# One transformer block on one core: the written order of four engines laid anew, and both ends of the program

## The reference, cut to what matters

```
x = x + layernorm(attention(layernorm(x)))          # q, k get a position table; causal softmax; Wo
x = x + layernorm(tanh(layernorm(x) @ W @ A1 @ A2 + bias))
attention: qkv = x @ Wqkv.T ; scores = q k.T / 8, masked ; probs = softmax ; (probs v) @ Wo.T
```

## Time and profile before

| what | before |
|---|---|
| median of three runs | 561.74 us |
| the profiled execution, its own time | 561.25 us |
| span of its trace (first to last instruction) | 559.4 us |
| busy: PE / PEld / DVE / ACT / POOL | 537.3 / 455.6 / 469.5 / 409.4 / 398.9 us |
| chain of work that ended last: PE share | 92% |
| granted TensorE clock, mean | 0.987 |
| load of a batch of x, 128 KB, issue to landing, median | 2.2 us |
| scores of batch 1, second pair, idle PE before, waiting for `qk` from DVE (L641) | 1.00 us |

### The profile page before, as it was taken

How to read it: one execution, slowest core, us unless ns; L and a number is a source line. 1 busy time by engine, 2 the same in 40 slices (tenths; PEclk the granted TensorE clock), 3 DMA queues, 4 the chain that set the end, 5 groups by cost and what they waited for, 6 DMA issues and landing times.

```text
span 559.4 us, 16795 instructions
## 1 busy us (share of the span) xinstructions
PE 537.3 (96%) x4595; PEld 455.6 (81%) x4595; DVE 469.5 (84%) x2063; ACT 409.4 (73%) x1507; POOL 398.9 (71%) x650
## 2 busy tenths in 40 slices
PE   7799999999999999999999999999999999999971
PEld 4588888888888888888888888888888888888850
DVE  4987898888889888888888888988888888888843
ACT  2777877778778777777877877777787787777740
POOL 3535777877777787777787777778777777776653
PEclk9999999999999999999999999999999999999985
DMA  5000011100000100000100010011000011100000
GB/s 160 29 2 21 11 30 30 30 19 28 20 18 28 28 28 19 28 17 21 28 28 25 22 28 9 28 28 28 19 28 24 14 28 28 28 9 21 21 9 19
DMA packets 27963, 14.53 MB, mean 26 GB/s; under 512 B 1700, under 2 KB 27431, under 8 KB 27943
## 3 DMA queue, kind: packets, MB, share of 16 engines
q1 hardware_dynamic: 27510, 13.51, 8.5%
q10 hardware_dynamic: 432, 0.79, 0.4%
HBM read 10.09 MB, written 4.19 MB: 26 GB/s over the span
## 4 chain that ended last, share of the span: by engine, by line
PE 92%; DVE 3%; ACT 2%; issue 1%; DMA 1%; POOL 1%; POOLq 0%; DVEq 0%; ACTq 0%
PE scores L879 18%; PE turned_and_heads L933 17%; PE misc_bank L994 11%; PE qk_bank L894 6%; PE qk_bank L896 5%; PE qk_bank L895 5%; PE turned_probs L910 5%; PE turned_probs L911 5%; PE turned_and_heads L919 5%; PE misc_bank L865 4%; PE misc_bank L977 3%; PE misc_bank L867 3%; PE misc_bank L866 3%; PE misc_bank L939 2%; PE misc_bank L975 1%
## 5 line engine op out<-in xcount | busy, mean ns | idle before, releaser
L263 ACT ACTIVATE probs<-scores,neg_max 128x256 f32<-128x256 f32 (+1 forms) x512 | 208.6, 425 | 43.4 <-DVE neg_max L631 43.3
L631 DVE CUSTOM_DVE_ANT_0 scores<-scores,mask 128x256 f32<-128x256 f32 (+1 forms) x512 | 166.2, 386 | 11.4 <-PE scores L879 11.4
L641 DVE TENSOR_TENSOR qk<-qk_bank,pe 128x512 f32<-128x512 f32 x128 | 87.4, 683 | 32.9 <-PE qk_bank L896 25.1
L421 POOL TENSOR_TENSOR probs<-probs,inv_sum 128x512 f32<-128x512 f32 x126 | 101.3, 823 | 12.6 <-DVE inv_sum L647 12.6
L879 PE MATMUL scores<-qk 64*128 64x256 f32 (+1 forms) x1024 | 106.6, 342 | 1.6 <-DVE qk L641 1.0
L263 ACT ACTIVATION_READ_ACCUMULATOR probs<-scores,neg_max 128x1 f32 x512 | 107.5, 210 | 0.0
L879 PEld LDWEIGHTS scores<-qk 64*128 64x128 f32 x1024 | 87.9, 186 | 18.7 <-issue 11.2
L933 PE MATMUL turned_and_heads<-pt,vals 128*64 128x256 f32 (+1 forms) x1024 | 98.5, 335 | 1.4 <-ACT pt L283 1.4
L933 PEld LDWEIGHTS turned_and_heads<-pt,vals 128*64 128x64 f32 x1024 | 64.6, 137 | 27.7 <-issue 2.0
L894 PE MATMUL qk_bank<-xt_hi,w_hi 128*128 128x256 f32 x256 | 80.5, 314 | 2.0 <-DVE qk L641 1.2
L281 ACT COPY pt<-turned_probs 128x512 f32<-128x512 f32 x128 | 76.4, 597 | 7.3 <-PE turned_probs L911 3.7
(11 more groups left out here) (91 smaller groups left out, 1013.8 us busy)
## 6 DMA issues: line engine op xcount, KB each, us to landing
x_in<-in_x SPq DMA_DIRECT2D x32, 128.0 KB, 2.2
x_res<-in_x SPq DMA_DIRECT2D x32, 128.0 KB, 2.1
out_x<-x SPq DMA_DIRECT2D x32, 128.0 KB, 1.8
w_raw<-in_w_qkv_t ACTq DMA_DIRECT2D x3, 256.0 KB, 3.8
pe<-pe_table SPq DMA_DIRECT2D x1, 256.0 KB, 5.2
wo<-in_w_o_t SPq DMA_DIRECT2D x1, 256.0 KB, 3.8
mask<-causal_mask SPq DMA_DIRECT2D x1, 128.0 KB, 5.3
w_sb<-in_w SPq DMA_DIRECT2D x2, 64.0 KB, 3.3
```

Of the source, the lines that this page charges most:

```text
L263: ins = nc.scalar.activation(probs[k][j][:, h, lo:hi], s_bank[j][:, h, lo:hi], ACT.Exp, bias=neg_max[k][j][:, i:i + 1], scale=-1.0, accum_ ...
L421: ins = nc.gpsimd.tensor_tensor(some, some, inv, ALU.mult)
L631: ins = nc.vector.tensor_tensor_reduce(some, some, mask[:, t * P:2 * P], -1.0, HIGHEST, ALU.add, ALU.min, neg_max[k][j][:, i:i + 1])
L641: nc.vector.tensor_tensor(qk[j][:, :], qk_bank[:, :], pe[:, :], ALU.add).then_inc(qk_kept, 1)
```

## The change

No arithmetic of a batch changes. The slots of all four engines get another order, the boundary between the slots moves, and the start and the end are written anew:

- PE: in the period the projection of b-1 moves behind the first `turn_probs(b, 0, 0)`, and the second `turn_probs(b, 0, 1)` comes right behind it; then `make_qk(b+1, 0, 1)`, and `make_vals(b+1, 0)` only after that. `make_heads` of unit 0 still stands right behind the next scores.
- DVE: the first `row_max` of unit 1 goes ahead of `keep_x_lo(b+1)` and of `scale_probs(b, 0)`; `stats_ffn` goes from k = 0 behind `stats_attn`; the moments of y follow `keep_heads`; a `drain` is dropped and replaced by a wait.
- POOL: `make_out(b-3)` goes ahead of `scale_probs(b, 0)`. ACT: `keep_y` ahead of `keep_x_hi`, `keep_turned(b, 0, 0)` ahead of `keep_attn`.
- Start: the first two thirds of the weights are loaded from SP's queue behind the first x, the last third, the mask and Wo from ACT's, after a first `Exp` on a tiny tile; 10 warming products instead of 12.
- End: the last projection goes into `qk_bank`, with no wait for `tanh`, ahead of the FFN of batch 30; the last scaling goes ahead of the copy of the heads; 4, 17 and 4 warming products stand among the last steps of PE. On DVE the statistics of `tanh` of batch 30 stand ahead of those of the last projection, as before; on ACT `keep_y` of batch 30 stands ahead of the last `keep_heads`, as before, while PE's `turn_y` of batch 30 moves behind `make_heads(31, 1)`.

```diff
@@ -213,9 +213,11 @@
                     sp.dma_start(rows(out_dram, c), x2[c.parity][:, :, :]).then_inc(stored[c.parity], 16)
             load(first, x_in, x_loaded)
+            for i in range(2):
+                part = slice(i * F, (i + 1) * F)
+                sp.dma_start(w_raw[:, part], w_qkv_t[:, part]).then_inc(w_in[i], 16)
             sp.dma_start(ident[:, :], ident_dram).then_inc(ident_in, 16)
             sp.dma_start(pe[:, :], pe_dram).then_inc(pe_in, 16)
-            sp.dma_start(mask[:, :], mask_dram).then_inc(mask_in, 16)
             load(first.plus(1), x_in, x_loaded)
             sp.wait_ge(zeros_set, 5)
...
@@ -241,9 +242,12 @@
         @block.scalar
         def _(act):
-            for i in range(3):
-                part = slice(i * F, (i + 1) * F)
-                act.dma_start(w_raw[:, part], w_qkv_t[:, part]).then_inc(w_in[i], 16)
+
+            act.wait_ge(zeros_set, 2)
+            nc.scalar.activation(touched[:, :], eps[:, :], ACT.Exp)
+            act.dma_start(w_raw[:, 2 * F:3 * F], w_qkv_t[:, 2 * F:3 * F]).then_inc(w_in[2], 16)
+            act.dma_start(mask[:, :], mask_dram).then_inc(mask_in, 16)
+            act.dma_start(wo[:, :, :], w_o_t.rearrange("(c f) e -> f c e", f=P)).then_inc(wo_in, 16)
             def round_w(i):
...
             def slot(b, k):
                 if k == 0:
-                    keep_turned(b.plus(-1), 0, 1)
                     keep_vals(b, 0)
                     exps(b, 0, 0)
                     keep_vals(b, 1)
                     keep_turned(b.plus(-1), 1, 0)
                     exps(b, 0, 1)
                     keep_turned(b.plus(-1), 1, 1)
-                    keep_x_hi(b.plus(1))
                     keep_y(b.plus(-2))
                 else:
+                    keep_x_hi(b.plus(1))
                     keep_heads(b.plus(-1))
                     tanh(b.plus(-2))
                     exps(b, 1, 0)
+                    keep_turned(b, 0, 0)
                     keep_attn(b.plus(-1))
-                    keep_turned(b, 0, 0)
                     exps(b, 1, 1)
+                    keep_turned(b, 0, 1)
...
@@ -482,15 +485,15 @@
             def slot(b, k):
                 if k == 0:
-                    rstd_attn(b.plus(-2))
-                    make_x1(b.plus(-2))
-                    scale_probs(b.plus(-1), 1)
-                    norm_y(b.plus(-2))
                     norm_ffn(b.plus(-3))
                 else:
+                    make_out(b.plus(-3))
                     scale_probs(b, 0)
-                    make_out(b.plus(-3))
                     norm_x(b.plus(2))
+                    rstd_attn(b.plus(-1))
+                    make_x1(b.plus(-1))
+                    scale_probs(b, 1)
+                    norm_y(b.plus(-1))
...
@@ -681,35 +680,35 @@
             def slot(b, k):
                 if k == 0:
+                    invert_sums(b.plus(-1), 1, 1)
                     norm_attn(b.plus(-2))
-                    invert_sums(b.plus(-1), 1, 1)
                     row_max(b, 0, 0)
                     stats_y(b.plus(-2))
-                    nc.vector.drain()
+                    wait_stats("y", b.plus(-2))
+                    keep_heads(b.plus(-1))
                     take_moments("y", b.plus(-2))
-                    keep_heads(b.plus(-1))
                     keep_qk(b, 1, 0)
                     row_max(b, 0, 1)
-                    stats_ffn(b.plus(-3))
                     wait_stats("ffn", b.plus(-3))
+                    stats_x(b.plus(2))
+                    take_moments("ffn", b.plus(-3))
+                else:
+                    wait_stats("x", b.plus(2))
+                    keep_qk(b, 1, 1)
+                    take_moments("x", b.plus(2))
                     invert_sums(b, 0, 0)
-                    take_moments("ffn", b.plus(-3))
-                    keep_qk(b, 1, 1)
-                    stats_x(b.plus(2))
+                    row_max(b, 1, 0)
+                    keep_x_lo(b.plus(1))
+                    invert_sums(b, 0, 1)
                     scale_probs(b, 0)
-                    invert_sums(b, 0, 1)
-                else:
-                    keep_x_lo(b.plus(1))
-                    row_max(b, 1, 0)
-                    wait_stats("x", b.plus(2))
+                    row_max(b, 1, 1)
                     keep_qk(b.plus(1), 0, 0)
-                    take_moments("x", b.plus(2))
-                    row_max(b, 1, 1)
+                    invert_sums(b, 1, 0)
+                    scale_probs(b, 1)
                     stats_attn(b.plus(-1))
                     wait_stats("attn", b.plus(-1))
-                    invert_sums(b, 1, 0)
+                    stats_ffn(b.plus(-2))
                     take_moments("attn", b.plus(-1))
-                    scale_probs(b, 1)
                     keep_qk(b.plus(1), 0, 1)
...
@@ -977,6 +976,17 @@
                     ins = mm(misc_bank[:, T + t * E:T + (t + 1) * E], yt[b.parity][:, t * P:(t + 1) * P], wf[:, :],
                              start=False, stop=True, skip_group_check=True)
                 ins.then_inc(ffn_made, 1)
+
+            def make_attn_last():
+
+                pe_eng.wait_ge(heads_kept[0], B)
+                pe_eng.wait_ge(heads_kept[1], B)
+                pe_eng.wait_ge(qk_kept, 4 * B)
+                for t in range(TT):
+                    for p in range(PAIRS):
+                        ins = mm(qk_bank[:, t * E:(t + 1) * E], heads_t[1][:, p, t * P:(t + 1) * P], wo[:, p, :],
+                                 start=(p == 0), stop=(p == PAIRS - 1))
+                ins.then_inc(attn_made, 1)
             def make_attn(b, t):
                 if not b.exists():
...
@@ -998,11 +1008,11 @@
             def slot(b, k):
                 if k == 0:
+                    make_heads(b.plus(-1), 0)
                     make_qk(b, 1, 0)
                     make_vals(b, 1)
                     turn_probs(b.plus(-1), 1, 0)
                     make_qk(b, 1, 1)
-                else:
                     turn_x(b.plus(1))
                     turn_probs(b.plus(-1), 1, 1)
                     turn_y(b.plus(-2))
@@ -1010,29 +1020,29 @@
                     make_heads(b.plus(-1), 1)
                     make_ffn(b.plus(-2))
                     make_qk(b.plus(1), 0, 0)
+                else:
+                    turn_probs(b, 0, 0)
                     make_attn(b.plus(-1), 0)
                     make_attn(b.plus(-1), 1)
-                    turn_probs(b, 0, 0)
+                    turn_probs(b, 0, 1)
+                    make_qk(b.plus(1), 0, 1)
                     make_vals(b.plus(1), 0)
-                    make_qk(b.plus(1), 0, 1)
-                    turn_probs(b, 0, 1)
                     make_scores(b.plus(1), 0)
-                    make_heads(b, 0)
-
-            def warm_up(n, columns=512):
+
+            def warm_up(n, bank, columns=512):
                 for _ in range(n):
-                    mm(qk_bank[:, 0:columns], warm[:, 0:P], warm[:, 0:columns], start=True, stop=True)
+                    mm(bank[:, 0:columns], warm[:, 0:P], warm[:, 0:columns], start=True, stop=True)
             def fuse(n, lhs, rhs):
                 mm(heads_bank[:, n * P:(n + 1) * P], lhs[:, :], rhs[:, :], start=True, stop=True).then_inc(fused_pe, 1)
...
                 turn_probs(last, 0, 1)
+                warm_up(4, qk_bank, 256)
                 make_heads(last, 0)
                 turn_probs(last, 1, 0)
                 turn_probs(last, 1, 1)
+                make_heads(last, 1)
                 turn_y(last.plus(-1))
-                make_heads(last, 1)
+                make_attn_last()
                 make_ffn(last.plus(-1))
-                make_attn(last, 0)
-                make_attn(last, 1)
+                pe_eng.wait_ge(exps_done, 4 * B)
+                warm_up(17, s_bank[0][:, 0, :])
                 turn_y(last)
+                warm_up(4, s_bank[0][:, 0, :], 256)
                 make_ffn(last)
```

More of the change, by code:

```diff
@@ L112, in build_block @@
         warm = sb("warm", [P, 512], BF16)
-        half_power, eps = sb("half_power", [P, TT]), sb("eps", [P, TT])
+        half_power, eps, touched = (sb(n, [P, TT]) for n in ("half_power", "eps", "touched"))
         def two(name, shape, dt=F32):
@@ L357, in end @@
             def end():
-                keep_turned(last.plus(-1), 0, 1)
                 keep_vals(last, 0)
                 exps(last, 0, 0)
+                keep_turned(last.plus(-1), 1, 0)
                 keep_vals(last, 1)
-                keep_turned(last.plus(-1), 1, 0)
+                exps(last, 0, 1)
+                keep_turned(last.plus(-1), 1, 1)
                 keep_y(last.plus(-2))
-                keep_turned(last.plus(-1), 1, 1)
-                exps(last, 0, 1)
+                exps(last, 1, 0)
+                keep_heads(last.plus(-1))
                 tanh(last.plus(-2))
-                keep_heads(last.plus(-1))
-                exps(last, 1, 0)
+                keep_turned(last, 0, 0)
+                exps(last, 1, 1)
```

(44 more changed lines are left out.)

12 lines of the change are left out of this document (5 added, 7 removed).

## The result

The changed kernel takes 568.3 us (median of 6 runs, 567.09 to 569.03) against 561.6 before (6 runs beside it): a ratio of 1.0123, with a 95% interval of 1.0107 to 1.0139. The forecast was 559.3 with a range of 549 to 566; the time lies outside the range, on the slower side, by the mechanism of the second rival, priced at 565, and by a start whose cost was put too low. The profiled execution has a span of 566.07 us against 559.44.

A forecast was written before the change was run, and what follows sets the result against it. The time was taken as PE's list plus the places where PE stands still. From 561.25, start +0.2, loop -1.5 (29 periods of -0.05) and end -0.8 gave 559.15, stated as 559.3 us; range 549 to 566.

The forecast's parts named there:

- the second rival: Slower: the chain heads, copy, moments, POOL's norm, turn of y delays each period; 565 us in total, chance of slower 0.26.
- Removed waits: PE's waits at the projection and the value products in each period both go: -0.43 us a period.
- Turn of pair 0: PE's first turn waits for DVE's scaling, lengthened by a POOL instruction let in: +0.34 us a period.
- Turn of y: PE's turn of y waits as y's moments now follow the heads' copy: +0.04 us a period, between 0 and 0.3.
- my own first term: In the turn of pair 0, DVE's scaling takes 1.86 us instead of 1.43, with POOL's first half let in.
- The start: Loads and first two batches in the new order: +0.2 us in sum, between -1.5 and +2.
- batch 0: Part of the start: rest of x, first turn and second turn wait in batch 0, less removed waits: +2.1 us (1 to 3).
- batch 1: Part of the start: a 1.00 wait in batch 1's scores goes, the second batch's turn waits 0.5 more: -0.9 us.
- The first part: Part of the start: x lands earlier, identity and weights are issued later: -1.0 us, between 0 and -1.3.
- The end: Last heads, scaling and projection gain, ACT's copy and DVE's statistics lose: -0.8 us in sum, between -2.5 and +1.
- POOL isn't let in: Rival: POOL stays out of DVE's scaling, pair 0's turn doesn't wait, period 16.02 to 16.07, total 549; whole gain chance 0.14.

The follow-up runs named there:

- experiment 1: Changed kernel with DVE's reciprocal of pair 1 of unit 0 moved behind its scaling of pair 0: 551.03 us, ratio 0.9802 to the kernel before.
- experiment 2: Changed kernel with POOL scaling the narrow half of pair 1 first and the wide one second: 553.3 us, ratio 0.9849 to the kernel before.
- experiment 5: Changed kernel with DVE's scaling ahead of the second reciprocal, and the start of the kernel before: 549.7 us, ratio 0.9784 to the kernel before.
- experiment 6: Changed kernel with DVE's scaling ahead of the second reciprocal, and 19 warming products instead of 10 at the start: 549.52 us, ratio 0.9786.
- experiment 3: Changed kernel with DVE taking the moments of y ahead of the copy of the heads again, with the old drain: 562.45 us, ratio 1.0008.
- experiment 4: Changed kernel with both DVE's scaling ahead of the second reciprocal and y's moments ahead of the copy of the heads: 550.73 us, ratio 0.9799.
- experiment 8: Changed kernel with scaling ahead of the second reciprocal, y's moments ahead of the heads' copy, and the old start: 548.98 us, ratio 0.9782.
- experiment 7: Changed kernel with DVE's scaling ahead of the second reciprocal, and no warming products at the end: 551.58 us, ratio 0.9828.

## Why the prediction was wrong, step by step

- **Removed waits, -0.43 a period: right.** Projection and values follow at their bare distances.
- **Turn of pair 0, +0.34: right.** Measured 0.385 in the mean; DVE's scaling 1.84 for 1.86 forecast. The mechanism, one POOL instruction let in between DVE's halves, is shown by experiments 1 and 2 from both sides.
- **Turn of y, +0.04: this is the step that failed.** It measured 0.25 in the mean (0.275 in the loop), within its bound of 0.3 but six times the value taken. I let this chain start at the copy of the heads where it stood in the old profile, released by PE, and argued that DVE would be in time. But my own first term made DVE's scaling 0.4 longer, and all that stands behind it on DVE came later: the attention's statistics, then POOL's `attn_rstd` (for which DVE idles 0.42), `attn_n`, the row maximum 0.3 late, the statistics of y, and so the copy, 0.3 late. The release by PE gave no shelter: even with the statistics at their old place DVE would have reached the copy only at 3.12 of the forecast's 3.13, so any delay on DVE had to show. Experiment 1 parts the 0.25: 0.16 hangs on the longer scaling, and 0.09 stays without it, from the new order itself. I had even written that `norm_attn` comes 0.4 later, and then used the old row's release. The second rival named this chain and priced it at 0.15 to 0.2 a period; it got 0.26 of the chance. The sum of the loop, by means over the 29 periods, is 16.448 - 0.433 + 0.385 + 0.25 - 0.055 = 16.595 (0.055 less is waited in the second unit's scores, which I had said would not swallow any of it), for 16.615 measured; the last 0.02 lies in the spacing of products at their new places.
- **The start, +0.2: wrong, +3.36.** The parts of batch 0 (+2.1 forecast, +2.49) and batch 1 (-0.9, -1.01) came out in size. For batch 0 that says little of its terms: with the first experiment's edit and a whole clock it is +1.51 (11.42 to 25.56 in experiment 5). The first part was -1.0 and measured +1.88. x did land 1.26 earlier, but that did not reach the scores, since the identity and the second third of the weights land later, the identity by 2.5 and not only by the one us of its issue: with the clock whole the first scores come at 11.44, -0.06. Of the other 1.95 some 0.2 is a later landing and the rest the clock, which I had weighed for the end and not for the start, where 10 warming products stood in front of a wait that I had myself made longer. Experiment 5 gives it back at the first scores; experiment 6 only in part there, but by the scores of batch 2 it is 1.06 ahead of experiment 1 (42.23 against 43.29; 41.19 in experiment 5).
- **The end, -0.8: right in sign, -1.58.** The clock held until 560.5 in the profiled run. Its size is partly luck: in experiments 1 to 6 and 8, which have the same end, the stretch behind the last scores takes 39.54 to 40.62 us, -1.62 to -0.54 against the kernel before (41.16), and without the warming products, in experiment 7, 40.32, which is -0.84. So the order of the heads and the attention is worth about that by itself; how its terms share it was not taken apart.
- **The range** reached 566 and left out 2.3 us. Its upper end came from the loop alone (the second rival's bound), though the start could go against me as well, and did. From the forecast sum of 559.15: loop +4.85 instead of -1.5 is +6.35, start +3.36 instead of +0.2 is +3.16, end -1.58 instead of -0.8 is -0.78; together 567.88, which is 561.25 + 6.63; the profiled execution's own time is 567.91.
- **The rivals.** "POOL isn't let in" (549) was nearly a true price: once it isn't, the kernel runs in 551.0 with a period of 16.072 (16.02 to 16.07 forecast), and in 549.0 to 549.7 where the clock at the start stays whole too (experiments 5, 6 and 8). The order of two lines decides between it and the slow side.
- The cited page, "SBUF — State Buffer", section "Who interferes with whom", of the Trainium skill, held: POOL's first half waits for DVE's first, and DVE's second half for POOL's. What the traces add is the size: one whole instruction of the other engine, once, 0.385 a period at pair 0; with POOL released behind DVE's scaling it is nothing.

## What to carry to other kernels

- Where DVE and POOL both multiply two tiles, do not release POOL's right ahead of DVE's: 0.09 us of reciprocal ahead of the scaling cost 17 us of 568 here. Put the release behind, or let the other engine's short instruction come first.
- When a term makes one engine later, move every row behind it before using that row in the next term. Two waits on one chain are not independent terms.
- At the start, count the idle time between warming and the first true product, and keep the engine busy until the load that it waits for, but not beyond: 19 products held the clock and made the turn of x 0.9 late.

## What the runs showed that I had not expected

The same start fell to half clock or not from one execution to the next: in the profiled executions idle times of 2.16, 1.62, 1.43 and 1.42 us in front of the turn of x stand ahead of a fall at 7.5 to 9.3 (changed kernel, experiments 1, 4 and 2), and one of 1.17 ahead of no fall (experiment 7). The kernels with another start wait 0.85, 0.37, 0.27 and not at all there, and none falls (the kernel before, experiments 8, 5 and 6). Experiment 3 waits 1.82, and its 256-column products take 0.41 to 0.42 from 9.7 on, though its clock records begin only at 13.7. And with the clock whole through batch 0, the later stretch at half speed (18.9 to 22.3 in experiment 1, 19.4 to 26.2 in experiment 4) did not occur either, though the waits in batch 0 were the same (0.89 and 0.74 us in experiment 5, 0.88 and 0.73 in experiment 1): it is not those waits alone that bring it on. Nor does the early fall alone: the changed kernel has it, and no later one before 560.5. What decides stays open.
